# Graph convolution by relation: 32 KiB for the descriptors of POOL's DMAs, and 60 ring slots instead of 100

## The reference, cut to what matters

```python
def _rgcn_conv(x, src, dst, et, basis, comp, root, bias):
    W = jnp.einsum('rb,bio->rio', comp, basis)
    xw = jnp.einsum('ni,rio->nro', x, W)
    msgs = xw[src, et]
    seg = dst * N_REL + et
    summed = jax.ops.segment_sum(msgs, seg, num_segments=N_NODES * N_REL)
    cnt = jax.ops.segment_sum(jnp.ones((msgs.shape[0],), x.dtype), seg, num_segments=N_NODES * N_REL)
    mean = summed / jnp.maximum(cnt, 1.0)[:, None]
    agg = mean.reshape(N_NODES, N_REL, HIDDEN).sum(axis=1)
    return agg + x @ root + bias
# twice: h = relu(_rgcn_conv(h, ...)) + h; then layernorm(x + h)
```

## Time and profile before

| | us |
|---|---|
| median of 3 runs (5050.7 to 5052.8) | 5051.21 |
| the profiled execution, its own time | 5047.87 |
| its span (first to last instruction) | 5046.1 |

### The profile page before, as it was taken

One profiled execution on the slowest core, in us unless ns is written; L12 is line 12 of the kernel. 1 busy time (PEld: TensorE's weight loads), 2 busy tenths in 40 slices (PEclk: granted clock), 3 DMA queues, 4 the chain that ended last, 5 costly groups with the idle time before them and its releaser, 6 DMA issues.

```text
span 5046.1 us, 91632 instructions
## 1 busy us (share of the span) xinstructions
PE 3255.1 (65%) x20895; PEld 3007.8 (60%) x20895; DVE 1839.1 (36%) x6662; ACT 2286.4 (45%) x6539; POOL 3838.0 (76%) x3447
## 2 busy tenths in 40 slices
PE   6277766666666666666676666666666666666667
PEld 4166665666555566655555656655665665656656
DVE  8444433333333333333333333333333333333335
ACT  4165544444444444444454444444444444444445
POOL 7877777777777777777767777777777777777775
PEclk9599988877888888888888887788778778887888
DMA  6111111111111111111121111111111111111114
GB/s 106 51 41 43 44 43 44 43 43 44 43 44 43 43 44 43 44 43 43 43 80 44 43 44 43 43 44 43 44 43 43 44 43 44 43 43 44 43 44 119
DMA packets 287032, 241.73 MB, mean 48 GB/s; under 512 B 164335, under 2 KB 238267, under 8 KB 286987
## 3 DMA queue, kind: packets, MB, share of 16 engines
q0 software_dynamic: 216448, 209.55, 16.7%
q10 hardware_dynamic: 32488, 15.69, 1.4%
q1 hardware_dynamic: 38051, 15.98, 1.2%
HBM read 224.50 MB, written 14.44 MB: 47 GB/s over the span
## 4 chain that ended last, share of the span: by engine, by line
POOL 55%; issue 42%; DMA 1%; DVE 1%; SPq 0%; PE 0%; ACT 0%; POOLq 0%; DVEq 0%; ACTq 0%
POOL ring L299 54%; POOL S L333 0%; DMA h_rows<-S 0%; DMA S<-counts,idxg 0%; SPq L366 0%; DMA ring<-x,idx 0%; DVE W L267 0%; ACT S L562 0%; PE bank L662 0%; DVE aggT L859 0%; PE bank L673 0%; POOL aggT L348 0%; DVE hT L890 0%; DMA onehot<-x 0%; DVE S L837 0%
## 5 line engine op out<-in xcount | busy, mean ns | idle before, releaser
L662 PE MATMUL bank<-onehot,rows 119*128 119x128 f32 x9856 | 1702.2, 328 | 1618.4 <-ACT rows L523 1456.4
L523 ACT ACTIVATE rows<-ring,relnorm 119x128 f32 x4928 | 1569.0, 389 | 2520.4 <-SPq L401 1755.2
L662 PEld LDWEIGHTS bank<-onehot,rows 119*128 119x128 f32 x9856 | 1476.1, 230 | 1811.1 <-issue 1040.4
L299 POOL DMA_INDIRECT ring<-x,idx x1600 | 1807.8, 1130 | 543.5 <-issue 526.6
L299 POOL DMA_INDIRECT ring<-h_rows,idx x1600 | 1762.5, 1102 | 537.4 <-issue 524.0
L849 DVE TENSOR_TENSOR onehot<-bank,relnorm 119x512 f32<-119x512 f32 x1232 | 851.4, 691 | 1764.5 <-issue 1266.3
L673 PE MATMUL bank<-S,W 128*128 128x128 f32 x9856 | 1488.4, 316 | 1.4 <-ACT S L505 1.4
L673 PEld LDWEIGHTS bank<-S,W 128*128 128x128 f32 x9856 | 1455.7, 234 | 1.8 <-ACT S L505 1.8
L859 DVE TENSOR_TENSOR aggT<-aggT,bank 128x16 f32 x4928 | 833.4, 169 | 1337.1 <-PE bank L673 843.1
L505 ACT ACTIVATE S<-bank 128x512 f32<-128x512 f32 x1232 | 708.0, 575 | 15.1 <-PE bank L662 14.8
L299 POOL DMA_INDIRECT ring<-h_rows,idx_rest x81 | 89.2, 1102 | 26.0 <-issue 26.0
(11 more groups left out here) (114 smaller groups left out, 587.2 us busy)
## 6 DMA issues: line engine op xcount, KB each, us to landing
ring<-x,idx POOLq DMA_INDIRECT x1600
ring<-h_rows,idx POOLq DMA_INDIRECT x1600
S<-x ACTq DMA_DIRECT2D x24, 256.0 KB, 4.0
h_rows<-S SPq DMA_DIRECT2D x24, 256.0 KB, 3.0
onehot<-x ACTq DMA_DIRECT2D x24, 256.0 KB, 3.4
out<-S SPq DMA_DIRECT2D x24, 256.0 KB, 3.2
idx<-srcT SPq DMA_DIRECT2D x64, 23.2 KB
ring<-x,idx_rest POOLq DMA_INDIRECT x81
```

The costliest lines, as they stand in the source:

```text
L299: g.indirect_dma_start(out=ring[0:R, slot * P:(slot + 1) * P], out_offset=None, in_=table, in_offset=bass.IndirectOffsetOnAxis(ap=index, a ...
L523: s.activation(rows[0:R, u % 2 * BATCH + k, :], ring[0:R, bass.ds(v[2 * k + 1], P)], ACT.Copy, scale=relnorm[0:R, 1, bass.ds(b * BATCH + k ...
L662: last = t.matmul(bank[2 * (u % 2) + k // 4][:, k % 4 * P:(k % 4 + 1) * P], rows[0:R, at, :], onehot[0:R, at, :], start=True, stop=True)
```

## The change

The scratch for POOL's DMAs is set to 32 KiB per partition. The ring has 60 slots: `HALF` becomes 30, `LAG` 50, `ROUNDS` 28 and `REST` 1, since 1681 = 28 x 60 + 1. The load of all but the last column of `idx_rest` goes, and so the wait for it counts one DMA instead of two.

```diff
-    RING = 100
+    RING = 60
     HALF = RING // 2
     FLIGHT = 10
     GROUP = 5
     LAG = RING - FLIGHT
     ROUNDS = TILES // RING
     REST = TILES - ROUNDS * RING
-    assert REST and ROUNDS >= 4 and HALF % FLIGHT == 0
+    assert REST == 1 and ROUNDS >= 4 and HALF % FLIGHT == 0
...
-                pool.wait_ge(rest_in, 32)
+                pool.wait_ge(rest_in, 16)
...
-                sp.dma_start(idx_rest[0:R, 0:REST - 1], srcT[:, ROUNDS * RING:FULL]).then_inc(rest_in, 16)
                 sp.dma_start(idx_rest[0:TAIL, REST - 1:REST], src_tail.rearrange("(p a) -> p a", a=1)).then_inc(rest_in, 16)
...
-    nc = bacc.Bacc("TRN2", target_bir_lowering=False, num_devices=1)
+    nc = bacc.Bacc("TRN2", target_bir_lowering=False, num_devices=1, dynamic_dma_scratch_size=32768)
```

## The result

| | before | after |
|---|---|---|
| median of four runs each, side by side (us) | 5050.95 (5049.7 to 5052.8) | 5017.47 (5016.4 to 5019.7) |
| the profiled execution: own time, span | 5047.87, 5046.1 | 5018.3, 5016.4 |
| POOL gathers between prologue and layer 0's end | 1581 | 1621 |
| long gaps in layer 0's stream, in layer 1's | 28, 30 | 0, 0 |

The ratio is 0.9934 (95% interval 0.9917 to 0.9951): the changed kernel is faster by 33 us. The forecast was 5056, "no change". The direction is wrong, and the time lies 20 us under the range.

What follows compares the result with a forecast made beforehand. POOL's gathers and issue gaps bound the kernel. Terms 56.3 - 16.0 - 17.1 = 23.2 us later in layer 0, less 18.3 in layer 1, gave +4.9; on the median 5051.21 that made 5056, range 5037 to 5094.

Steps and rivals of the forecast that it cites:

- So 29 go: POOL's gather streams: doubled store removes 29 of 58 refreshes (long gaps read as store filling, being taken back), gaining 35.4 us.
- the interval goes from 55 to 110 gathers: POOL's streams: a doubled descriptor store makes refreshes come every 110 gathers, the first after 112, instead of every 55.
- The price: POOL's refresh: taken as 1.22 us each even when twice as many gathers are taken back; upper end 2.44.
- Rival 3: POOL's refresh is a wait for a late gather, found landed with twice the room: -30.5 us, 5021; chance 0.13.
- Rival 1: POOL's refresh price follows the number taken back, 22 ns per gather: up to +40 us, 5092; chance 0.30.
- Rival 2: POOL's store is not enlarged in use, the period stays 55 gathers: +41.5 us, 5093; chance 0.07.
- Rival 4: 60 slots stall POOL at the start of layer 0's stream: +42 us, 5093; chance 0.06.
- The smaller ring: Prologue: 40 gathers move into layer 0's stream, costing 56.3 us, against pairs starting 16 us earlier.
- The pairs: Prologue: POOL's 40 gathers of pairs, set by the tables landing, begin 16 us earlier than 201.09; ends 14.5 and 19.
- The rounds: VectorE's prologue chain: 12 more rounds at 0.474 us add 5.7 us, so the tables land 5.7 us later.
- The tables' stores: ACT's prologue stores, without ring gathers beside them, land at 178.8 instead of 180.5, and 184.5 with 5.7 us of added rounds.
- Costed at nothing: Slot reuse, index loads, removed `idx_rest` load and smaller memset, the tail, and 12 more POOL loop turns: no cost each.

Runs made afterwards that it cites:

- the fourth question: Guarded kernels, clock 0.71 to 0.73: 100 slots, 16,640 bytes, two or five gathers per semaphore (5834.0, 5858.9 us); changed kernel with two (5834.0) or five (5842.5).
- the changed kernel with the guard: Changed kernel plus ACT's and SP's wait values masked with 4095 and an empty SP instruction before its wait on ACT: 5842.5 us, ratio 1.0116, at reduced clock.

## Why the prediction was wrong, point by point

**The step that failed** is "So 29 go", which charges the 29 refreshes that stay 1.22 us each: 58 went, and the full stores of the changed kernel cost nothing (no gap over 0.31 us). The rows of before showed a long gap at every full store, and the prediction took full store and gap for one thing. They are two. The step ahead of it, "the interval goes from 55 to 110 gathers", holds: the nine faint gaps of the fourth question show the 110 (and 113, not 112, ahead of the first). But by the reach rule such a store keeps three gathers instead of one, so what it waits for has landed. The interval of exactly 55 was the hint: it is 56 - 1, and a whole number of groups, and the prediction took note of neither. Doubling is not what helps: 8, 15.5, 17, 18 and 24 KiB do it as well, 20, 23 and 30 don't.

**The price.** 1.22 us was nearly right for the old store (1.26 from the gaps themselves; in layer 1's sum the prediction has 1851.4 us of busy time where 1762.5 + 89.2 is 1851.7, worth 0.01 in the price). The choice of "the same" for twice the number fell: near 110 it would be 1.9 us by the slope above. At 30 KiB 30 gaps of 1.84 are 55 us of the old 73, a saving of 18 where the fixed price says 36.

**The rivals.** Rival 3 gave 5021, within 4 us of the result, and its sign was the point: the gap is in part a wait for a landing. But its mechanism, "with twice the room finds it landed", isn't what happens; at 30 KiB there is nearly twice the room and the gap is longer. Its counterargument in the prediction, that twice the store doesn't change what has landed just ahead, is sound and stopped one step short: which gather the store's size leaves as the last taken back does change it. Rival 1 was right that the price grows with the number taken back (by 0.012 us each, half of its 22 ns), and it tells at 20, 23 and 30 KiB, not here, where nothing is paid. Rival 2 fell: the interval follows the store in every run that shows one. Rival 4 fell: POOL waits 14.9 us for SP in all.

**The smaller ring** held. 40 more gathers are 56.3 us as forecast. The pairs start at 183.07, 18.0 us earlier, for a forecast of 16 (14.5 to 19). The rounds cost what was said: the timeline of VectorE after has its last L801 and its last step of the counts at

```profile
83.22 0.18 DVE L801 TENSOR_TENSOR tmpg<-tmpg 128x20 f32<-128x20 f32 x1
...
166.24 1.93 DVE L822 COPY_PREDICATED aggT<-aggT 125x1600 f32<-125x1600 uint32 x1
```

The rounds begin 2.1 us earlier than in the earlier trace rows and last 5.6 us longer, so the counts end 3.5 us later, not 5.7; that is most of the 2 us. The tables' stores without the gathers beside them:

```profile
180.00:181.00 1.00, 0.59 (x2) 0.00 (x0) 0.00 (x0) 0.83 (x2) 0.00 (x0) 1.00 0.30 128
181.00:182.00 1.00, 0.00 (x0) 0.00 (x0) 0.00 (x0) 0.32 (x1) 0.00 (x0) 1.00 0.19 77
182.00:183.00 1.00, 0.00 (x0) 0.00 (x0) 0.00 (x0) 0.00 (x0) 0.00 (x0) 1.00 0.00 0
```

They land by 182, 14 us behind the counts' end at 168.17, for 16 before. "Costed at nothing" held for slot reuse, index loads, the tail and the loop turns, with two small misses: 1.4078 us a gather for 1.4065, 4.6 us over both layers, and 0.6 in the tail.

**The sums.** With the right count the prediction's own working gives 4.9 - 29 x 1.22 = -30.5, and the profile shows -29.7. That they meet within 1 us is in part luck: the start 2.1 us earlier than forecast and the price of 1.26 for 1.22 (58 times, 2.2 us) are made up by the period's 4.6 and the tail's 0.6. No other term was off by more than 5 us.

## What to carry to other kernels

A periodic gap on the engine that sets the time is worth an experiment on its phase before one on its size: look at which other period (here the gathers that share a semaphore) its interval is a whole number of. Where POOL issues thousands of small indirect DMAs, try a store a little larger or smaller, or more semaphores with fewer DMAs each. Here 512 bytes less brought 74 us and two to a semaphore 80 in one run, and both left the ring its 100 slots; the change under study paid 38 us of ring for the same.

## What the runs showed of the hardware that was not expected

- In these runs a full store cost POOL nothing visible where by the reach rule it keeps two or more gathers (exactly two was run only on the chip at 0.72), and 1.25 to 1.84 us where it keeps one; one was kept only with two semaphores in turn. Of the two parts of that time only the wait for the landing and the slope are shown; where the work runs while nothing is visible isn't. In the runs at 0.72 it became visible when POOL had been held up just before (gaps of 0.69 to 0.72 us at 50 taken back, 0.51 to 2.03 at 106, 0.33 to 0.41 at 110), so it seems to run ahead of the issue; why being held up exposes it, and by such different amounts, stays open.
- The plain period was 1.408 us in the 60-slot runs without gaps and at 20 KiB, 1.4065 in the other 60-slot runs on a chip with a POOL bound and in all runs with 100 slots there. Nothing run here explains the 0.1%.
- At a granted clock near 0.72 the kernel before takes 5771 us for 5050. In that condition the changed kernel with the guard was 1.2% slower than the one before, and its POOL waited 778 us for SP instead of setting the pace. Whether the ring, the guard or the missing gaps do it wasn't separated (100 slots, 57 gathers held and no refresh gap took 5858.9 in one run, so it isn't the ring alone); the gain of 33 us is shown only for a chip on which POOL sets the time.
